# Decoder layer on one core: attention's inverse sums spread beside the scores, contexts copied by ScalarE, row peaks by chunk, keys and values made earlier

## The reference, cut to what matters

```python
q = x_q @ W_q.T + b_q
k = x_kv @ W_k.T + b_k
v = x_kv @ W_v.T + b_v
scores = jnp.einsum('bhqd,bhkd->bhqk', qh, kh) * scale
attn = jax.nn.softmax(scores, axis=-1)
ctx = jnp.einsum('bhqk,bhkd->bhqd', attn, vh)
return ctx @ W_out.T + b_out
# the feed-forward needs for each row
scale = 127.0 / jnp.clip(jnp.max(jnp.abs(x), axis=-1, keepdims=True), 1e-05)
```

## Time and profile before

| | |
|---|---|
| median of 3 runs | 718.6 us (718.55 to 720.26) |
| profiled execution | 719.91 us, span of the trace 718.1 us |
| granted TensorE clock, mean | 0.989 of full speed |
| PE busy | 673.4 us, 94% of the span |
| DVE busy | 631.8 us, 88% |
| ACT, POOL busy | 372.8 us (52%), 353.1 us (49%) |
| hyena | 0 to about 450.5 us |
| attention | 450.8 to about 597 us, steady loop from 483 to 588 us |
| feed-forward | from about 597 us |

### The profile page before, as it was taken

The page is one execution under the profiler, slowest core; times in us unless marked ns, Lnnn a source line. Parts: engine busy times, 40 slices in busy tenths (PEclk is TensorE's granted clock), DMA queues, the critical chain, the costliest instruction groups (busy, mean ns, idle before and its releaser), DMA issues. The chain is left out here.

```text
span 718.1 us, 12542 instructions
## 1 busy us (share of the span) xinstructions
PE 673.4 (94%) x4396; PEld 494.7 (69%) x4412; DVE 631.8 (88%) x1257; ACT 372.8 (52%) x720; POOL 353.1 (49%) x491
## 2 busy tenths in 40 slices
PE   9889999999989998899979899899999999999995
PEld 3478765887747886468866686567777876666663
DVE  4998787999989999989999788558999997999997
ACT  3732157021264502464112723679767776988885
POOL 0633424646045761258431561580692223788785
PEclk9999999999999999999989999999999999999999
DMA  8630045321331536143382077810000000000012
GB/s 308 180 60 1 0 118 112 74 50 28 61 58 31 131 109 71 23 78 79 113 113 64 1 194 136 298 56 2 2 2 2 2 2 1 1 31 31 31 60 89
DMA packets 35112, 50.31 MB, mean 70 GB/s; under 512 B 4744, under 2 KB 29192, under 8 KB 34794
## 3 DMA queue, kind: packets, MB, share of 16 engines
q0 software_dynamic: 7680, 16.77, 14.9%
q1 hardware_dynamic: 26506, 31.95, 13.4%
q10 hardware_dynamic: 864, 0.79, 0.4%
HBM read 29.59 MB, written 7.34 MB: 51 GB/s over the span
## 5 line engine op out<-in xcount | busy, mean ns | idle before, releaser
L705 ACT ACTIVATE yb<-banks 128x256 f32<-128x256 f32 x64 | 24.2, 386 | 156.9 <-PE banks L427 110.5
L450 PE MATMUL banks<-xt_in,w_in 128*128 128x512 f32 x192 | 87.8, 611 | 0.2
L418 PE MATMUL banks<-inv_m,spec_y 128*128 128x256 f32 x384 | 86.8, 383 | 0.0
L375 PE MATMUL banks<-z_cplx,fwd_m 128*128 128x256 f32 x240 | 72.3, 383 | 9.7 <-DVE prod L1078 5.4
L418 PEld LDWEIGHTS banks<-inv_m,spec_y 128*128 128x128 f32 x384 | 74.2, 193 | 10.3
L376 PE MATMUL banks<-z_cplx,fwd_m 128*128 128x256 f32 x240 | 71.4, 379 | 0.0
L450 PEld LDWEIGHTS banks<-xt_in,w_in 128*128 128x128 f32 x192 | 36.7, 194 | 42.8 <-issue 39.5
L375 PEld LDWEIGHTS banks<-z_cplx,fwd_m 128*128 128x128 f32 x240 | 44.8, 190 | 18.9 <-issue 8.4
L376 PEld LDWEIGHTS banks<-z_cplx,fwd_m 128*128 128x128 f32 x240 | 45.7, 191 | 6.1
L2016 DVE TENSOR_REDUCE peak<-ps_score 128x16 f32<-128x1024 f32 x32 | 38.2, 1194 | 8.2 <-PE ps_score L1501 8.2
L1742 ACT ACTIVATE silu<-ps_score,gate_back 128x1024 f32<-128x1024 f32 x32 | 35.6, 1113 | 18.7 <-issue 17.6
(11 more groups left out here) (292 smaller groups left out, 1725.0 us busy)
## 6 DMA issues: line engine op xcount, KB each, us to landing
x_tok<-in_x SPq DMA_DIRECT2D x8, 512.0 KB, 4.4
x_tok<-in_b_out POOLq DMA_DIRECT2D x8, 512.0 KB, 13.3
v_t<-left POOLq DMA_DIRECT2D x8, 511.5 KB, 4.6
x_t<-left POOLq DMA_DIRECT2D x8, 511.5 KB, 5.3
xt_in<-in_x_t SPq DMA_DIRECT2D x3, 1024.0 KB, 5.9
x_scratch<-x_tok SPq DMA_DIRECT2D x6, 512.0 KB, 4.1
x<-x_scratch SPq DMA_DIRECT2D x6, 512.0 KB, 9.3
out<-x SPq DMA_DIRECT2D x6, 512.0 KB, 2.9
```

The lines of the kernel that those rows point to most:

```text
L375: mm(o, fwd_m[:, at + 2 * half + odd, :], zz[:, 0, :], start=True, stop=False)
L418: last = mm(bank[:, odd * 2 * P:(odd + 1) * 2 * P], spec_y[:, j + odd, part * D + h * P:part * D + (h + 1) * P], inv_m[:, o:o + 2 * P], st ...
L450: last = mm(proj_pair(b, t)[:, c * 512:(c + 1) * 512], w_in[:, k, TILES[t] * P:(TILES[t] + 1) * P], xt_in[:, k, c * 512:(c + 1) * 512], st ...
```

## The change

Keys and values are made in hyena's last batch between `inv(u, 0)` and `inv(u, 1)`, their operands loaded by seven DMAs before the query weights'; attention loads six operands in place of fifteen and begins with `scores(0)`. The order of the first tiles' chunk work is evened out. For i = 0 to 13 (`BESIDE` = 14) the spread inverses are made by 32-row strips into columns 256 to 383 of the four score banks, in the middle of `turn_prob`; ACT copies the contexts instead of the spread inverses; DVE multiplies the copy by the score banks' columns. New waits go with it. DVE inverts ahead of the residual. Row peaks are taken for four tiles at once, from j = 14 on.

```diff
@@ hyena @@
+            sp.wait_ge(proj_done, T_ALL * B)
+            for dst, src in context_loads(d, xt_in, w_in):
+                sp.dma_start(dst, src).then_inc(ld_ctx, 16)
             sp.wait_ge(*convolved(B - 1, T_ALL - 1))
...
+            def keys():
+                pe.wait_ge(ld_ctx, 16 * CTX_LOADS)
+                for t in range(DT):
+                    for k in range(DT):
+                        last = mm(FB[0][:, t * B * NCTX:(t + 1) * B * NCTX], wk[:, k, t * P:(t + 1) * P], ctx_2[:, k, :, 0, :],
+                                  start=(k == 0), stop=(k == DT - 1))
+                last.then_inc(context_mm, 1)
...
             def batch(b, last_one, first):
                 u = 2 * b
                 inv(u, 0, first)
+                if last_one:
+                    pe.wait_ge(prod_done, 8 * (u + 1))
+                    keys()
+                    for n in range(B // 2):
+                        values(n)
...
                 inv(u, 1)
                 if last_one:
-                    pe.wait_ge(prod_done, 8 * (u + 1))
+                    pe.wait_ge(context_evac, DT + B // 2)
                     turn_rows(0, FB[0:2])
...
@@ attention, PE @@
+        BESIDE = HALVES - 2
+        spread_at = score_banks[:, :, DT * P:DT * P + P]
...
             def scores(j):
...
+                if j % 2 and j >= 5:
+                    pe.wait_ge(ct_ready, (j - 5) // 2 + 1)
...
-                last.then_inc(s_mm, 1)
+                if j % 2 or j < 4:
+                    last.then_inc(s_mm, 1)
+
+            def spread_beside(i):
+
+                pe.wait_ge(inverted, i + 1)
+                for g in range(STRIPS):
+                    rows = slice(g * STRIP, (g + 1) * STRIP)
+                    last = mm(spread_at[:, g, :], spread[rows, g, :], inv_sum[rows, :], start=True, stop=True)
+                last.then_inc(s_mm, 1)
 
             def turn_prob(j):
...
                 for h in range(PAIRS):
+                    if h == PAIRS // 2 and j % 2 and j // 2 - 1 in range(BESIDE):
+                        spread_beside(j // 2 - 1)
                     if h % (PAIRS // 2) == 0:
...
-            make_values(0, 2)
-            scores(0)
-            make_values(2, B)
-            turn_x(Q_EARLY)
+            scores(0)
             for j in range(TILES_ALL):
                 if j + 1 < TILES_ALL:
                     scores(j + 1)
-                if j == 0:
-                    queries(Q_EARLY)
-                if j == 2:
-                    turn_x(Q_EARLY + 2)
+                if Q_EARLY + j < CHUNKS:
+                    turn_x(Q_EARLY + j)
                 turn_prob(j)
...
+                if Q_EARLY + j < CHUNKS:
                     queries(Q_EARLY + j)
@@ attention, ACT @@
+            def evac_contexts(i):
+
+                act.wait_ge(pv_mm, i + 1)
                 if i:
                     act.wait_ge(ct_ready, i)
-                fn(inv_all[:], ps_inv[:], ACT.Copy).then_inc(inv_evac, 1)
+                fn(inv_all[:], ps_ctx[:], ACT.Copy).then_inc(inv_evac, 1)
@@ attention, DVE @@
             def normalize(i):
+                if i < BESIDE:
+                    dve.wait_ge(s_mm, 2 * i + 5)
                 dve.wait_ge(inv_evac, i + 1)
                 dve.wait_ge(pv_mm, i + 1)
...
+                if i < BESIDE:
+                    tt(c_t[:].rearrange("p t (k n) -> p t k n", k=2), spread_at.rearrange("p (k t) n -> p t k n", t=DT),
+                       inv_all[:].rearrange("p (t k n) -> p t k n", t=DT, k=2), ALU.mult).then_inc(ct_ready, 1)
...
+            def x_peaks(c):
+                of = slice(c * CH, (c + 1) * CH)
+                dve.wait_ge(x2_ready, c + 1)
+                reduce(x_peak[:, of], x2[:, of, :], AX_X, ALU.max, apply_absolute_value=True).then_inc(x_peaked, CH)
...
                 shift(j)
...
                 i = j // 2 - 1
                 if j % 2:
+                    if i >= 0:
+                        invert(i)
                     if i >= 1:
                         add_residual(i - 1)
-                    if i >= 0:
-                        invert(i)
                 elif i >= 1:
                     normalize(i - 1)
+                c, k = divmod(j - X_LATE, CH)
+                if c in range(X_EARLY) and k == 0:
+                    x_peaks(c)
+                    x_scales(c)
```

More of the change, by code:

```diff
@@ L551, in queries, with values @@
                     last.then_inc(query_mm, 1)
+            def keys():
[5 more added lines that the diff above has]
+                last.then_inc(context_mm, 1)
+            def values(n):
+                for b in (2 * n, 2 * n + 1):
+                    for k in range(DT):
+                        last = mm(FB[1 + n][:, b % 2 * D:(b % 2 + 1) * D], ctx_2[:, k, b].rearrange("p r n -> p (r n)"), wv[:, k, :],
+                                  start=(k == 0), stop=(k == DT - 1))
+                last.then_inc(context_mm, 1)
             def batch(b, last_one, first):
@@ L761, in evac_queries, with evac_context @@
                        bias=bq[:, t:t + 1]).then_inc(query_evac, 1)
+            def evac_context():
+                for t in range(T_ALL - 3, T_ALL):
+                    act.wait_ge(*convolved(B - 1, t))
+                act.wait_ge(context_mm, 1)
+                for t in range(DT):
+                    fn(k_t[:, t].rearrange("p b n -> p (b n)"), FB[0][:, t * B * NCTX:(t + 1) * B * NCTX], ACT.Identity,
+                       bias=bk[:, t:t + 1]).then_inc(context_evac, 1)
+                for n in range(B // 2):
+                    act.wait_ge(context_mm, n + 2)
+                    fn(raw_values(left, n), FB[1 + n][:, :], ACT.Copy).then_inc(context_evac, 1)
             def batch(b, last_one, first):
@@ L1253 @@
 X_ROWS = CHUNKS - CHUNKS_B
-X_LATE, X_EARLY = 12, 5
+X_LATE, X_EARLY = 14, 5
 W_TILE = 11
@@ L1267, in attention_operands @@
 def attention_operands(area, small):
-    area = area[:].rearrange("p k n -> p (k n)")
     small = small[:].rearrange("p t n -> p (t n)")
[L1271 to L1276, removed]
+    wo = None
+    if area is not None:
+        wo = area[:].rearrange("p k n -> p (k n)")[:, 0:DT * D].rearrange("p (t n) -> p t n", t=DT)
     bo, bv = small[:, 0:D], small[:, D:2 * D]
@@ L1284, in attention_operands, with raw_keys, raw_values, context_operands @@
     spread = small[:, o:o + STRIPS * P].rearrange("p (g n) -> p g n", n=P)
-    assert o + STRIPS * P <= DT * 3 * D
-    return w, ctx_t, ctx_2, pair_mask, key_head, spread, bo, bv, bk
+    o += STRIPS * P
+    bq = small[:, o:o + DT]
+    assert o + DT <= DT * 3 * D
+    return wo, pair_mask, key_head, spread, bo, bv, bk, bq
 def query_weights(left):
-    return left[:, 2, 0:DT * D].rearrange("p (t n) -> p t n", t=DT), left[:, 2, DT * D:DT * D + DT]
-def attention_loads(d, area, small):
[L1295 to L1300, removed]
+    return left[:, 2, 0:DT * D].rearrange("p (t n) -> p t n", t=DT)
+def raw_keys(left):
+    return left[:, 2, HALF:2 * HALF].rearrange("p (t b n) -> p t b n", t=DT, b=B)
+def raw_values(left, n):
+    return left[:, n, HALF:2 * HALF]
+def context_operands(xt_in):
+    flat = xt_in[:].rearrange("p t n -> p (t n)")
+    wk, wv = (flat[:, n * DT * D:(n + 1) * DT * D].rearrange("p (t n) -> p t n", t=DT) for n in range(2))
+    ctx_2 = flat[:, 2 * DT * D:2 * DT * D + 2 * DT * B * NCTX].rearrange("p (t b r n) -> p t b r n", t=DT, b=B, r=2)
+    return wk, wv, ctx_2
+def context_loads(d, xt_in, small):
+    wk, wv, ctx_2 = context_operands(xt_in)
+    bk = attention_operands(None, small)[-2]
+    ctx_src = d["ctx_t"].rearrange("(t p) (b n) -> p t b n", p=P, n=NCTX)
+    loads = [(ctx_2[:, t, :, r], ctx_src[:, t]) for t in range(DT) for r in range(2)]
+    loads += [(w, d[n].rearrange("(t p) n -> p t n", p=P)) for w, n in ((wk, "wk_t"), (wv, "wv_t"))]
+    loads += [(bk, d["bk"])]
+    assert len(loads) == CTX_LOADS
+    return loads
+def attention_loads(d, area, small):
+    wo, pair_mask, key_head, spread, bo, bv, bk, bq = attention_operands(area, small)
+    loads = [(wo, d["wo_t"].rearrange("(t p) n -> p t n", p=P))]
     loads += [(pair_mask, d["c_pairmask"].rearrange("p (h n) -> p h n", n=NCTX)),
@@ L1329, in psum @@
             return ctx.enter_context(nc.psum_tensor(name, [P, cols], F32))
-        (wk, wv, wo), ctx_t, ctx_2, pair_mask, key_head, spread, bo, bv, bk = attention_operands(area, small)
+        wo, pair_mask, key_head, spread, bo, bv, bk, bq = attention_operands(area, small)
         x2 = sb("x2", [P, TILES_ALL, D])
@@ L1446, in _ @@
             mm, transpose = nc.tensor.matmul, nc.tensor.transpose
[L1449 to L1462, removed]
             def turn_x(c):
@@ L1635, in _ @@
             pe.wait_ge(w_seq, 9)
+            pe.wait_ge(ct_ready, BESIDE)
             inner(0, ps_gate, w_gate, silu_done, gate_mm)
```

94 lines of the change are left out of this document (47 added, 47 removed).

## The result

The changed kernel takes 748.02 us (median of 4 runs, 746.67 to 748.39); the kernel before took 719.0 beside it. The ratio is 1.0393, 95% interval 1.0381 to 1.0406: slower by 3.9%. The forecast was 734.0 with a range up to 743. The direction and the closed loop were right; the size was not.

The account below looks back on a forecast made before the run. PE, with DVE nearly as full, was taken to bound attention's loop. Terms +17.0 (loop), -2.7 and +1.2 (start), -0.1 (hyena) gave +15.4 on 719.91: 735.3, or 734.0 us against the median; range 727 to 743.

Parts of the forecast that it names:

- the closed loop: Attention: scores(odd), turn_prob, project, sums on PE, then invert, residual, shift(even), normalize on DVE set a pair's least time, 9.37 us.
- The clock falls in attention's new idle time: Rival: 1.8 us idle on PE per pair lowers the clock in most pairs, 1.77 us each; 752 us; chance 0.10.
- one longer stretch that kept its speed: Evidence against clock falls: 2.44 us of PE idle time, full products behind it, was not followed by slow work.
- The pair: Two tiles in attention's loop: 9.37 us against 8.09 before; 13 of them, with weights' totals, add 17.0 us.
- The bound of 0.89: Upper price of the spread on PE in attention, its old time; 0.33 was taken; 0.89 would add 0.43 a pair.
- DVE's order: Attention's loop: DVE inverts, then adds the residual, 0.69 us, before shift(even); counted as a term of the 9.37 us.
- The second rival: Attention: PE's work, not the loop of waits, sets the time; 0.56 us saved in each of 14 pairs; 708 us; chance 0.05.
- Peaks: Attention, DVE: 20 reductions of 0.41 us become 5 of 1.22, hidden in idle time; value 0, bounds -1 to +2 us.
- Start: Attention's beginning: -2.7 us up to sums(0), with the exponential 2.5 us earlier, then +1.2 us from sums(0) to scores(5).
- Hyena's last batch: Keys and values fill PE's 4.54 us wait; inv(u, 1) ends 2.3 us sooner, but PE waits for DVE's gate: -0.1 us.

## Why the prediction was right in kind and wrong in size

**The closed loop: right.** scores(odd) wait for `c_t` in each pair, with 1.71 us of idle time for 1.8. A plain pair is 9.46 where 9.37 was forecast. One wait alone made 9.02 to 9.07, and without the waits and with the old order it is 8.0 to 8.1.

**The step that failed: "The clock falls in attention's new idle time", held for a rival with a chance of 0.10.** The sum of the forecast had nothing for it. Six of 13 pairs fell, 1.68 us each (priced at 1.77), 9.2 us of the loop against the same loop without falls. All three ways of filling the idle time took the falls away and gave 8.8 to 10.3 us. The forecast weighed it as all or nothing, "in most pairs" or in none, and let one longer stretch that kept its speed speak against it. The profiles say how to read that: the two stretches of 1.96 us in the middle batches were both followed by a fall in the profile of before (3.65 and 3.29 us for 1.98); after, with the same instructions and the same idle time, the first was (3.37) and the second wasn't (1.98). Over the twelve profiles whose hyena is unfilled, these two stretches were followed by a fall 16 times in 24. The stretch of 2.44 us that "kept its speed" fell as well in three of the fourteen profiles, the run with one product among them:

```profile
40.92 0.70 PE L382 MATMUL banks<-z_cplx,fwd_m 128*128 128x256 f32 x2 [2.44 <-DVE z_cplx L1052]
...
42.59 1.06 PE L383 MATMUL banks<-z_cplx,fwd_m 128*128 128x256 f32 x2
```

Such a pair of records takes 0.59 otherwise. So the same stretch falls in one execution and not in the next, one profile couldn't speak against the falls, and 13 stretches of 1.7 us should have carried some falls in the forecast itself: at one in two, 11 us. In the loop it was 12 of 26, with the run that put the order back, and never in two pairs running.

**The pair, 0.09 short.** From start to start: scores(odd) to invert 4.56 us (forecast 4.65), invert 0.87 (0.88), residual to shift(even) 0.80 (0.69), shift 2.40 (2.40), normalize and the way back 0.83 (0.75). The longer residual step is the spread. It takes 0.43 to 0.50 where 0.33 was taken, and the transposes cut in two by it take 0.59 each against 0.51: 1.61 us in place of 1.35. That moves PE's side of shift(even) from 1.5 to 1.74 us behind sums (547.57 to 549.31), as late as DVE's side. The bound of 0.89 was never near. The Trainium skill (page "TensorEngine Tiling (Array Packing)", section "Key Properties") says that a change of tiling mode drains TensorE; the 0.16 us more for the same transposes agree, though no run separates a drain from the rest. In all 13 pairs 124.1 without falls in place of 122.1: 1.1 from this, 0.9 from the sixth pair. That the chain shows contexts and ACT's copy in place of `invert` and `x` is the same near tie: the copy ends at 551.57, `c_t` starts at 551.78, 0.2 later (forecast 0.3).

**DVE's order: priced rightly in this loop, and its cost hidden.** The forecast put the residual between invert and shift(even) at 0.69. Moving it out gains nothing here, since the spread ends with it, but in the old loop that place costs 8.4 us. The forecast read the chain of before as having no DVE step in a pair. That holds up to 523 us; from 523.42 to 531.48 the same chain is DVE's (`c_t`, `peak`, `prob`, the row peaks, `x`, `inv_sum`, `peak`, `prob`), right ahead of the earlier trace rows, so DVE had next to no slack to give. The second rival, PE as the bound at 708, could not have happened with this order even without the waits.

**Peaks: right here (0), wrong as a statement on the old loop.** The pairs of the changed kernel are 9.46 with and without chunk peaks, but for the sixth, where a chunk's small operation was held up; in the old loop they cost 2.5 us, just past the upper bound of +2.

**Start: -1.88 for -2.7, then +1.40 for +1.2.** The first exponential starts at 454.51 against 458.39, with hyena's 1.40 taken off the 2.5 us of the forecast; from there to sums(0) it is 20.6 us, not 19.8. The step left out is the clock: in the old loop, the filled start gave back 1.7 us between scores(0) and scores(5). **Hyena's last batch: -0.25 for -0.1**, and PE's wait for the gate came as described.

Sum on the profiled runs, forecast +15.4: falls +9.2, pairs +2.0, start +0.8 and +0.2, rest +0.2, unchanged hyena -1.15, last batch -0.15: +26.5. The median of the runs is 1.35 above the profiled one, about as much as one more fall would be.

**Left open.** Whether spreading beside the scores could pay with fewer waits wasn't tried: DVE reads the spread inverses out of the banks that the next scores write, the forecast took both waits as needed, and no run leaves one out of the changed kernel. How the falls are spread over the pairs (the second, fourth, sixth, ninth, eleventh and last) isn't explained by any run, nor is what decides whether a stretch falls.

## What to carry to other kernels

Work taken from a full engine at the price of a wait back to it is read round the loop: the wait closed a cycle through PE, DVE and PE, and a pair cost the cycle's length, not PE's sum. Idle time on PE that recurs in each period is priced with some falls of the clock in the forecast itself, and it can be bought back with products nobody reads. Before believing that a reordering or a merged operation is free, ask what stands behind it in that engine's list: two swapped lines cost 8.4 us, and one 1.2 us reduction in place of four short ones 2.5.

## What the runs showed of the hardware that was not expected

A small DVE operation that started while POOL worked on 128x2048 ended only when POOL's did. In the changed kernel (DVE, then POOL):

```profile
533.03 1.57 DVE L2127 TENSOR_SCALAR x_unit<-x_peak 128x4 f32<-128x4 f32 x1
```
```profile
532.67 1.90 POOL L1939 TENSOR_SCALAR w_raw<-w_raw 128x2048 f32<-128x2048 f32 x1
```

The first ends 0.03 us after the second; elsewhere it takes 0.17. The same came in the runs without waits (1.74), with one wait (1.37) and with one filler product (1.56), where that pair took 10.32 in place of 9.46, and on a small scale in the kernel before (0.41). The Trainium skill (page "SBUF — State Buffer", section "SBUF: two separate sides") says that GpSimd and some DVE operations, those in a 2-port mode or with two inputs in SBUF, share one pair of ports, which the one that starts first holds for its whole instruction. The trace agrees for this operation, while a reduction over 128x1024 at 531.79 took its usual 1.21 beside POOL's 1.97 us from 530.62. Which mode the operation ran in, no trace here shows.
